# Gated linear attention and expert feed-forward on one core: epsilon on POOL, attention matrix with chunks innermost, two pairs of level banks

## The reference, cut to what matters

```python
# x: (16, 512, 256); H = 4 heads, key width 64 and value width 128 per head
x = x + layernorm(attn(layernorm(x)))
x = x + layernorm(ffn(layernorm(x)))          # layernorm: (x - mean) / sqrt(var + 1e-5)

# attn
q = (x @ Wq) * 64 ** -0.5; k = x @ Wk; v = x @ Wv
g = log_sigmoid(x @ gk_w1 @ gk_w2 + gk_b) / 16
# for each head, token by token:
S = exp(g_t)[:, None] * S + k_t[:, None] * v_t[None, :]
o_t = q_t @ S
o = o * rsqrt(mean(o * o) + 1e-5) * rms_w
attn = (o * silu(x @ Wg)) @ Wo

# ffn: 8 experts, each for 2 of the 16 sequences
ffn = gelu(tokens @ w1[e] + b1[e]) @ w2[e] + b2[e]
```

## Time and profile before

| | us |
|---|---|
| median of 3 runs | 1315.18 (1313.88 to 1315.83) |
| the profiled execution | 1313.97 |
| its span | 1312.2 |
| PE, DVE, ACT, POOL busy | 1230.2, 1044.8, 711.3, 635.0 |
| largest DVE groups | copies into `attn_T` 152.7 in 160, q updates 141.3 in 192 |
| PE's level matmuls | 241.1, idle before them 26.4 |

### The profile page before, as it was taken

The page is one execution under the profiler, slowest core; times in us unless marked ns, Lnnn a source line. Parts: engine busy times, 40 slices in busy tenths (PEclk is TensorE's granted clock), DMA queues, the critical chain, the costliest instruction groups (busy, mean ns, idle before and its releaser), DMA issues. The chain is left out here.

```text
span 1312.2 us, 23418 instructions
## 1 busy us (share of the span) xinstructions
PE 1230.2 (94%) x8372; PEld 1073.7 (82%) x8372; DVE 1044.8 (80%) x2404; ACT 711.3 (54%) x1443; POOL 635.0 (48%) x893
## 2 busy tenths in 40 slices
PE   5889999999999999999999999999999999999957
PEld 3677889888897888889888788988889888897956
DVE  3769788796978979787787978879697896978863
ACT  5365555656456465644756555565545646465423
POOL 5436353563445544564435635356354554456431
PEclk9989999999999999999999999999999999999988
DMA  3110010100101001010011001010010100100000
GB/s 97 38 33 17 17 49 1 54 17 17 49 21 49 1 17 49 21 49 1 17 49 53 16 17 49 1 54 16 17 49 21 48 2 17 49 21 33 1 17 17
DMA packets 31778, 38.27 MB, mean 29 GB/s; under 512 B 2448, under 2 KB 29104, under 8 KB 31664
## 3 DMA queue, kind: packets, MB, share of 16 engines
q1 hardware_dynamic: 31136, 36.25, 8.3%
q10 hardware_dynamic: 528, 0.52, 0.1%
HBM read 28.38 MB, written 8.39 MB: 28 GB/s over the span
## 5 line engine op out<-in xcount | busy, mean ns | idle before, releaser
L1047 POOL TENSOR_TENSOR k_decayed<-k_decayed,block_totals 128x256 f32<-128x256 f32 x192 | 168.2, 876 | 277.1 <-PE ps_level L298 276.6
L298 PEld LDWEIGHTS ps_level<-q_blockdiag,k_decayed 128*128 128x128 f32 x1792 | 227.1, 191 | 51.5 <-DVE q_blockdiag L585 41.1
L298 PE MATMUL ps_level<-q_blockdiag,k_decayed 128*128 128x128 f32 x1792 | 241.1, 278 | 26.4 <-DVE q_blockdiag L585 25.1
L575 DVE COPY_PREDICATED attn_T<-level_masks,ps_level 128x512 f32<-128x512 uint32 x160 | 152.7, 954 | 16.0 <-PE ps_level L298 16.0
L585 DVE TENSOR_TENSOR q_blockdiag<-q_blockdiag,block_totals 128x512 f32<-128x512 f32 x192 | 141.3, 736 | 28.1 <-PE ps_level L298 28.1
L1053 POOL TENSOR_TENSOR rstd<-rstd,minus_half 128x1 f32<-128x1 f32 x192 | 111.7, 584 | 106.6 <-DVE rstd L636 106.6
L255 PE MATMUL ps_big<-w_ff_hi,h_hi 128*128 128x256 f32 x512 | 150.1, 293 | 3.0 <-DVE h_lo L590 3.0
L257 PE MATMUL ps_big<-w_ff_hi,h_lo 128*128 128x256 f32 x512 | 144.8, 283 | 0.0
L256 PE MATMUL ps_big<-w_ff_lo,h_hi 128*128 128x256 f32 x512 | 144.7, 283 | 0.0
L837 ACT ACTIVATE gelu_out<-ps_big,ff_b_cols 128x512 f32<-128x512 f32 x128 | 88.0, 688 | 79.8 <-PE ps_big L257 43.2
L623 DVE SCALAR_TENSOR_TENSOR o<-o,o_rstd,out_gate 128x128 f32<-128x128 f32 x256 | 93.3, 426 | 45.0 <-POOL o_rstd L1068 45.0
(11 more groups left out here) (113 smaller groups left out, 3155.1 us busy)
## 6 DMA issues: line engine op xcount, KB each, us to landing
w_raw<-L_ffn_w SPq DMA_DIRECT2D x16, 1024.0 KB, 5.6
out<-y SPq DMA_DIRECT2D x16, 512.0 KB, 2.9
x_in<-L_attn_x SPq DMA_DIRECT2D x15, 512.0 KB, 3.9
ff_b_rows<-L_ffn_b SPq DMA_DIRECT2D x8, 128.0 KB, 2.6
x_in<-L_attn_x ACTq DMA_DIRECT2D x1, 512.0 KB, 4.0
w_raw<-L_attn_Wv SPq DMA_DIRECT2D x1, 512.0 KB, 6.0
w_raw<-L_attn_Wg SPq DMA_DIRECT2D x1, 512.0 KB, 7.1
y<-L_attn_Wo SPq DMA_DIRECT2D x1, 512.0 KB, 8.1
```

What stands on the lines that cost most here:

```text
L298: last = nc.tensor.matmul(PL[tl][:, c * CH:(c + 1) * CH], kk[:, tl, c * CH:(c + 1) * CH], q[:, :, :, 1, :], start=True, stop=True)
L575: nc.vector.copy_predicated(dst, m.to_broadcast([P, 2 * NCH, HC // h, h]), src)\
L1047: nc.gpsimd.tensor_tensor(k, k, t.to_broadcast([P, n, h]), ALU.mult)\
```

## The change

Four things, in one edit.

1. Epsilon: `stats_eps` becomes `stats`, without the add; POOL adds epsilon itself, in front of the power, with a wait of its own between the two (semaphores `po_e1` to `po_e4`).
2. `attn_T` is laid out with the four chunks innermost. The predicated copy writes runs of 4h floats, and reads the bank and the mask so; ACT's block copies write in steps of four floats; `att(c)` reads its weights in steps of four floats.
3. Levels use `PL` and, for odd i, `PO` and `PS`: a level waits for the copy two levels back. Row sums and diagonal move to `PT[0]` and `PT[1]`: `diag_rows` ahead of level 0, `diag_columns` behind it, and `x3t(1)` waits for DVE's copy of the diagonal. On DVE `q_update` comes first, the copy of the step before behind it.
4. POOL's `weight_lo(1, ...)` moves from steps 1 to 4 to steps 5 to 8.

```diff
-        Am = sb("attn_T", [P, KT, NCH * 2, CH])
+        Am = sb("attn_T", [P, KT, 2, CH, NCH])
...
+        LVB = [PL, [PO, PS]]
...
                 def level(i, tl):
-                        if i - 1 < MASKED:
-                            pe.wait_ge(sem["dv_cp"], at("dv_cp", s, 2 * (i - 1) + tl + 1))
-                        else:
-                            pe.wait_ge(sem["ac_cp"], at("ac_cp", s, 2 * tl + 2))
+                        if i >= 2:
+                            pe.wait_ge(sem["dv_cp"], at("dv_cp", s, 2 * (i - 2) + tl + 1))
...
                 def diag_rows():
-                            last = nc.tensor.matmul(PO[32 * c:32 * (c + 1), 0:CH], ind[:, tl, :],
+                            last = nc.tensor.matmul(PT[0][32 * c:32 * (c + 1), 0:CH], ind[:, tl, :],
...
                 def x3t(kt):
+                    if B and kt:
+                        pe.wait_ge(sem["dv_dg"], at("dv_dg", s, 1))
...
                 def st(c):
+                    pe.wait_ge(sem["ac_cp"], at("ac_cp", s, 6))
...
                 def att(c):
-                        last = nc.tensor.matmul(PO[:, w], Am[:, tl, 2 * c + hh, :], v[:, c, w],
+                        last = nc.tensor.matmul(PO[:, w], Am[:, tl, hh, :, c], v[:, c, w],
...
                 for step in range(2 * NL):
                     if B:
+                        if step == 0:
+                            diag_rows()
                         level(step // 2, step % 2)
                         if step == 1:
-                            diag_rows()
-                        if step == 3:
                             diag_columns()
...
                 def copy_pairs(i, tl):
-                    dst = Am[:, tl, :, :].rearrange("p a (n t h) -> p a n t h", t=2, h=h)[:, :, :, 1, :]
-                    src = PL[tl][:, :].rearrange("p (a n h) -> p a n h", a=2 * NCH, h=h)
-                    m = masks[:, i, :].bitcast(U32).rearrange("p (a n h) -> p a n h", a=1, h=h)
+                    dst = Am[:, tl, :, :, :].rearrange("p a (n t h) c -> p a n t h c", t=2, h=h)[:, :, :, 1, :, :]
+                    src = LVB[i % 2][tl][:, :].rearrange("p (c a n h) -> p a n h c", c=NCH, a=2, h=h)
+                    m = masks[:, i, :].bitcast(U32).rearrange("p (c a n h) -> p a n h c", c=1, a=1, h=h)
...
-                def stats_eps(k, src, c, name, b):
+                def stats(k, src, c, name, b):
...
-                    nc.vector.tensor_scalar(rs[:, k, c:c + 1], mv[:, k, c, 1:2], EPS, None, ALU.add)\
-                        .then_inc(sem[name], 1)
...
                 for step in range(2 * NL):
                     if B:
-                        if step // 2 < MASKED:
-                            copy_pairs(step // 2, step % 2)
                         q_update(step // 2, step % 2)
...
+                    if B and 1 <= step <= 2 * MASKED:
+                        copy_pairs((step - 1) // 2, (step - 1) % 2)
...
                 def copy_blocks(i, tl):
+                    act.wait_ge(sem["dv_cp"], at("dv_cp", s, 2 * MASKED))
...
                 def rsqrt(k, c, ready, b, name):
+                    nc.gpsimd.tensor_scalar(rs[:, k, c:c + 1], mv[:, k, c, 1:2], EPS, None, ALU.add)\
+                        .then_inc(sem[eps], 1)
+                    pool.wait_ge(sem[eps], at(eps, b, c + 1))
...
-                    if C and j == 1 and 1 <= step < 5:
-                        weight_lo(1, step - 1, e)
+                    if C and j == 1 and 5 <= step < 9:
+                        weight_lo(1, step - 5, e)
```

67 lines of the change are left out of this document (39 added, 28 removed).

## The result

The changed kernel takes 1379.5 us (median; 1377.6 to 1381.3) against 1315.3 us before (1313.9 to 1315.8): ratio 1.049, 95% interval 1.047 to 1.051. It is 64 us slower, where 2.3 us faster was forecast (1311.7 against the profiled execution's 1313.97); the range (1298 to 1350) did not hold it, and the rival that came nearest (strided weights, 1369) had been given a chance of 0.10.

A forecast was written before the change was run, and what follows sets the result against it. Bound: TensorE, busy 94% of the span, with 25.1 us of waits for VectorE's q_update. Seven even sequences at 0.1, eight odd at 1.05 less 1.1, first 2.0: 1313.97 - 2.3 = 1311.7 us; range 1298 to 1350.

The forecast's parts named there:

- Strided weights: att's 512 weight loads of attn_T in steps of four floats: forecast to cost nothing.
- the bound's 57: Upper bound for att's strided weight loads: at half pace 111 ns more each, 57 us over 512 loads.
- rival 3: att's weight reads in steps of four floats pay 57 us on PE's path: 1369 us; chance 0.10.
- Copies of 0.70 at all levels: VectorE's ten copies out of PSUM: 0.70 us each, where levels 0 and 1 took 1.33.
- the first sequence only (2.0 us): First sequence, no f1 between levels, VectorE sets the pace: four faster copies gain 2.0 us, bounds 0 and 4.
- The front: Sequence start up to third level: 8.5 us against 8.63 even and 9.57 odd, gaining 0.1 and 1.05.
- the 4.5 above: Time after the start at which dv_dg, VectorE's copy of the diagonal, was forecast: about 4.5 us.
- the four operations through the shared way: Front: k_update 0.85, q_update 0.55, k_update 0.7, q_update 0.55 us, run one after the other across VectorE and POOL.
- Epsilon: Add moved to POOL: VectorE freed of 0.22 us each, x_normed some 0.5 us later before the levels; cost nothing.
- Steps 5 to 8: Weight subtractions moved there: last h_lo 1.1 us later in each odd sequence, nothing in even; bounds 0 and 2.5.
- the 2.75 us step: Odd sequences, steps 5 to 8: q_update, k_update, h_lo and a subtraction take 2.75 us in a 2.28 us step.
- the forecast's own case: VectorE and POOL two-input operations serialise, copies take 0.70, weights free: 1311.7 us, own range 1303 to 1320; chance 0.45.

The follow-up runs named there:

- the run with five steps: Kernel before, att weights read in steps of 1, 2, 3, 4 and 8 floats (other numbers multiplied): loads 191, 199, 257, 319, 328 ns; no run time given.
- neighbouring reads: Changed kernel, but att reads 128 neighbouring columns as weights, so no strided weight read (other numbers multiplied, not usable): 1330.7 us, ratio 1.011.
- repacking once: Kernel before with chunks innermost, then ScalarE and VectorE each copy one half into neighbouring columns for att, chunk totals kept: 1295.7 us, ratio 0.984.

## Why the prediction was wrong, step by step

**Strided weights: the step that failed.** The prediction reads "I take nothing, the nearer row: a weight column goes in at 0.87 ns, while the f1 matmuls stream one in 0.46, so the read of weights has room." The price was 120 to 130 ns a load, 61 us in all, 49 net, close to the bound's 57. Two things were wrong with the choice. The row behind "no cost" was a step of two floats, of the operand that the level matmuls stream and not of their weights, and the price begins above two; the run with five steps shows it. And the pace at which the f1 matmuls stream says nothing about the read of weights. The rule of the Trainium skill, page "SBUF — State Buffer", section "SBUF: two separate sides", stood in the prediction as rival 3; the measurement agrees with it.

**Copies of 0.70 at all levels: right**, with the PSUM read in steps of 128 floats free. What they are worth was mis-sized. The forecast gave them the first sequence only (2.0 us), because it had reordered DVE so that copies were off PE's path, and never asked what fast copies do in the old order. There they are worth 32 us, more than all the reordering. In the first sequence the changed order got 0.3 of the 2.0 (66.24 us for 66.52, with neighbouring reads): half level by half level it is up to 1.8 us ahead, but the last one is only 0.9 earlier and att 0.4.

**The front: the right number by the wrong working.** Third level at 8.5, measured 8.57; the wait for dv_dg 1.4, measured 1.37. But two errors cancel in it: PE resumed behind the diagonal at 4.90, where the sum had 4.55, and needed 3.67 from there, where it had 3.97. And the working put q_update behind a k_update, at 2.57, and said of epsilon "Already in the 4.5 above". In the trace it began at 2.74, behind x_normed; with epsilon on VectorE it began at 1.78, ahead of k_update. So x_normed held the front, not the four operations through the shared way. Epsilon on POOL, priced at nothing there, was worth 0.94 us a sequence at that place, and 10 to 12 us wherever the clock did not take it back. That the number fitted proved nothing about the step.

**Epsilon: "x_normed comes some 0.5 us later" was short in size and wrong in path.** It came 0.88 us later in the kernel before and 0.87 in the changed one, and in the changed one it then ran 0.55 longer, beside POOL's k_update. It was costed against the transposes alone, which row sums covered. VectorE's queue behind x_normed was left out.

**Steps 5 to 8: the 2.75 us step was right** (in the changed kernel's timeline q_update starts at 784.58, 787.34 and 790.09), PE's last wait for h_lo grew by 1.7 us in an odd sequence (0.51 to 2.17) where 1.1 was forecast. It was put down to the weight subtractions; they hold 0.87 of it, and give 0.54 back at the front, so that moving them back gave only 0.25 us a sequence. The forecast had nothing in even ones, where 0.65 was measured. The missing path is ScalarE's: its block copies had been costed with "nothing", though they now wait for VectorE's last copy and take 1.3 us ahead of gelu 7. That is 0.4 us of the wait in either kind of sequence.

**Sum of the forecast's own case:** 1311.7 with the weights free, measured 1330.7. So even without the failed step the case would have missed, on the side of slower. Between the profiled executions of the kernel before and of that one, even sequences are 0.8 us longer (5.6 in seven), odd ones 0.66 (4.6), three falls of the clock take 4.5 and the last sequence with what follows it 2.7; the first sequence gives 0.3 where 2.0 was forecast.

## What to carry to other kernels

Keep what a weight load reads at no more than two floats from one column to the next. Two chunks innermost gave 1304.4 us with no other edit. If an evacuation wants a wider interleave, repacking once can give more (1295.7), but look at what the moved work then meets on the other engines. Price a faster operation first in the order that exists, before building a new order around it. And when a trace names the last arrival of a wait, go back along that engine's queue until something waited: the cause can stand there, as epsilon did ahead of the diagonal's copy.
